# Equal-target matrices of two mean stages of a graph kernel: made once and kept in DRAM, with new orders for four stages

## What is computed

```python
edge_index = jnp.stack([src, dst])
h = jnp.maximum(_layernorm(x, axis=-1), 0.0)
x = x + _L0_gnn_ref(h, edge_index, edge_weight)
h = jnp.maximum(_layernorm(x, axis=-1), 0.0)
x = x + _L1_gnn_ref(h, edge_index, ...)     # two mean convolutions
h = jnp.maximum(_layernorm(x, axis=-1), 0.0)
x = x + _L2_gnn_ref(h, edge_attr_2, ..., edge_index)
h = jnp.maximum(_layernorm(x, axis=-1), 0.0)
x = x + _L3_gnn_ref(h, edge_index, ...)
```

```python
def _sage_conv(x, src, dst, W_l, W_r, b, num_nodes):
    msgs = x[src]
    agg = jax.ops.segment_sum(msgs, dst, num_segments=num_nodes)
    deg = jax.ops.segment_sum(jnp.ones((src.shape[0],), x.dtype), dst, num_segments=num_nodes)
    agg = agg / jnp.maximum(deg, 1.0)[:, None]
    return agg @ W_l.T + b + x @ W_r.T
```

## Time and profile before

| | us |
|---|---|
| median of 3 runs (5081.73 to 5089.31) | 5084.06 |
| the profiled execution | 5089.15 |
| its span, from the first to the last instruction | 5087.2 |
| setup and `gcn_phase`, in the span | 0 to 1262 |
| first mean stage | 1262 to 1956 |
| second mean stage | 1956 to 2623 |
| edge-MLP stage | 2623 to 3629 |
| `mean_phase` | 3629 to 4313 |
| `final_phase` | 4313 to 5087 |

### The profile page before, as it was taken

The page is one execution under the profiler, slowest core; times in us unless marked ns, Lnnn a source line. Parts: engine busy times, 40 slices in busy tenths (PEclk is TensorE's granted clock), DMA queues, the critical chain, the costliest instruction groups (busy, mean ns, idle before and its releaser), DMA issues. The chain is left out here.

```text
span 5087.2 us, 85226 instructions
## 1 busy us (share of the span) xinstructions
PE 3758.1 (74%) x21809; PEld 2963.0 (58%) x22119; DVE 4106.7 (81%) x20428; ACT 3646.0 (72%) x9165; POOL 3840.9 (76%) x3164
## 2 busy tenths in 40 slices
PE   6537787876767778988868788778778777766564
PEld 4326666655655666776646666566566565645443
DVE  7659999988999997877778888878699898756564
ACT  0048898987777777877768788788678786766564
POOL 7777888875777777888766777776578886777777
PEclk9868999998888889999989899999899898877777
DMA  8977777776666666776668888888456565333332
GB/s 252 320 215 212 191 197 200 204 188 151 166 156 154 153 139 148 166 157 155 135 160 249 241 242 245 231 238 205 123 134 138 132 144 104 102 93 94 95 96 68
DMA packets 837876, 864.12 MB, mean 170 GB/s; under 512 B 89656, under 2 KB 621174, under 8 KB 837382
## 3 DMA queue, kind: packets, MB, share of 16 engines
q1 hardware_dynamic: 512124, 566.02, 34.5%
q0 software_dynamic: 219520, 232.07, 26.6%
q10 hardware_dynamic: 105738, 60.56, 4.3%
HBM read 339.16 MB, written 523.51 MB: 170 GB/s over the span
## 5 line engine op out<-in xcount | busy, mean ns | idle before, releaser
L1238 POOL DMA_INDIRECT node<-sage_comb,leadd x392 | 639.4, 1631 | 184.0 <-DMA node<-sage_comb,leadd 89.1
L474 PE MATMUL dense_p<-ident,dense_h 128*128 128x128 f32 x1956 | 335.4, 299 | 362.1 <-ACT dense_h L468 352.7
L468 ACT ACTIVATE dense_h<-dense_x,dense_n_shift,dense_n_rstd 128x128 f32<-128x128 f32 x1304 | 533.8, 486 | 74.5 <-DVE dense_n_shift L457 73.7
L474 PEld LDWEIGHTS dense_p<-ident,dense_h 128*128 128x128 f32 x1956 | 235.8, 151 | 459.1 <-ACT dense_h L468 439.3
L1238 POOL DMA_INDIRECT sums<-mlp_same,leadh x196 | 327.6, 1671 | 136.9 <-issue 63.7
L484 PE MATMUL dense_p<-wT,dense_hT 128*128 128x128 f32 x2608 | 375.0, 291 | 51.7 <-ACT dense_hT L1076 21.8
L1238 POOL DMA_INDIRECT node<-gcn_comb,leads x196 | 325.5, 1661 | 98.0 <-issue 39.1
L1238 POOL DMA_INDIRECT sums<-mean_comb,leads x196 | 321.9, 1642 | 92.1 <-DMA sums<-mean_comb,leads 42.7
L484 PEld LDWEIGHTS dense_p<-wT,dense_hT 128*128 128x128 f32 x2608 | 376.6, 208 | 20.7 <-issue 6.2
L1073 ACT ACTIVATE dense_hT<-dense_p 128x512 f32<-128x512 f32 x489 | 284.9, 587 | 61.5 <-PE dense_p L474 60.7
L465 ACT ACTIVATE dense_n_std<-dense_n_mean_var,eps 128x4 f32<-128x4 f32 x652 | 188.4, 293 | 153.6 <-DVE dense_n_mean_var L451 150.1
(11 more groups left out here) (322 smaller groups left out, 13889.1 us busy)
## 6 DMA issues: line engine op xcount, KB each, us to landing
node<-b SPq DMA_DIRECT2D x392, 256.0 KB
sums<-zero_row SPq DMA_DIRECT2D x392, 256.0 KB
node<-zero_row ACTq DMA_DIRECT2D x49, 1152.0 KB, 15.0
dense_x<-in_x SPq DMA_DIRECT2D x163, 256.0 KB
out<-dense_y SPq DMA_DIRECT2D x163, 256.0 KB
x_src<-xs SPq DMA_DIRECT2D x49, 256.0 KB, 5.8
y_dst<-gcn_y SPq DMA_DIRECT2D x49, 256.0 KB, 3.5
sage_xs<-x_src SPq DMA_DIRECT2D x49, 256.0 KB
```

What stands on the lines that cost most here:

```text
L468: tiles(lambda t: nc.scalar.activation(out[:, t, :], x[:, t, :], func, bias=b.sh[:, t:t + 1], scale=b.rs[:, t:t + 1])).then_inc(done, 1)
L474: return tiles(lambda t: nc.tensor.transpose(ps[:, t * P:(t + 1) * P], x[:, t, :], ident))
L1238: pool.indirect_dma_start(table, bass.IndirectOffsetOnAxis(ap=leads[:, i * G + c, t:t + 1], axis=0), e.comb[c][:, t, :], None, element_off ...
```

## The change

The first mean stage gets a step `put_same` on SyncE after `match`: it stores the six matrices of a chunk (768 KB) in a new DRAM tensor `same_dst`. `lead` of the next round on the same buffer waits until that has landed. The second mean stage loses `spread`, `krow` and `match` and gets `get_same` on SyncE: the matrices of the next round's chunk are loaded once `combine` is done with the buffer, those of the first round at the stage's start. `combine` waits for the load. 49 stores and 49 loads of 768 KB are added, 38.5 MB each way.

```diff
@@ Tables
+        self.same = dram("same_dst", (NCH, P, (T + U) * HALF), F32)
@@ planner
-AHEAD = ("fetch", "get_keys", "get_xs", "get_h", "get_x", "get_g", "get_side")
+AHEAD = ("fetch", "get_same", "get_keys", "get_xs", "get_h", "get_x", "get_g", "get_side")
@@ sage1_phase
-                    Node("spread", TENSOR, 560), Node("krow", SCALAR, 500), Node("lead", VECTOR, 2500), ...
+                    Node("spread", TENSOR, 560), Node("krow", SCALAR, 500), Node("lead", VECTOR, 2500, after=(("put_same", 1, 0),)), ...
-                 + edge_tail(True, SCALAR, whole=True) + fill_nodes(FILL))
+                 + edge_tail(True, SCALAR, match_after=(("put_same", 1, 0),), whole=True)
+                 + [Node("put_same", SYNC, 1400, after=(("match", 0, 0),), main=False)] + fill_nodes(FILL))
+                if name == "put_same":
+                    sp.wait_ge(e.done[c], at.after(i, "match"))
+                    sp.dma_start(chunk_rows(tb.same, i, c), e.same[c][:, :, :].rearrange("p b q -> p (b q)")).then_inc(kept_same[c], 16)
+                sp.wait_ge(kept_same[c], RDS[c] * 16)
+                if name == "lead":
+                    wait_rounds(dve, kept_same[c], i, 16)
@@ sage2_phase
-                 + [Node("spread", TENSOR, 560), Node("krow", SCALAR, 500)]
-                 + edge_tail(True, VECTOR, whole=True) + fill_nodes(FILL))
+                 + [Node("combine", TENSOR, 2850, after=(("get_same", 1, 0),)), Node("sumT", VECTOR, 610), Node("apply", TENSOR, 1000),
+                    Node("keep", SCALAR, 590, after=(("add", 1, 0),)),
+                    Node("add", GPSIMD, 2 * ADD, after=(("keep", 0, 0),), main=False, adds="table"),
+                    Node("get_same", SYNC, 1400, after=(("combine", 0, 0),), main=False)] + fill_nodes(FILL))
+            def load_same(i, c):
+                sp.dma_start(e.same[c][:, :, :].rearrange("p b q -> p (b q)"), chunk_rows(tb.same, i, c)).then_inc(e.krow_in[c], 16)
+                if name == "get_same" and not is_last(i, c):
+                    sp.wait_ge(e.done[c], at.after(i, "combine"))
+                    load_same(i + 1, c)
             for c in L:
                 load_p(0, c)
+                load_same(0, c)
-                if name == "match":
-                    match_keys(nc, dve, k, e, i, c, KD, field(k, i, c, INVD))
-                if name == "krow":
-                    act.wait_ge(e.done[c], at.before(i, name))
-                    nc.scalar.activation(e.krow[c][:, :], e.p[c][:, :], ACT.Copy).then_inc(e.done[c], 1)
-                if name == "spread":
-                    pe.wait_ge(e.done[c], at.before(i, name))
-                    spread_keys(nc, k, e.p[c], i, c, KD).then_inc(e.done[c], 1)
                 if name == "combine":
+                    pe.wait_ge(e.krow_in[c], (i + 1) * 16)
@@ TIMES
-    "sage2": (90922, 38122, (
+    "sage2": (84249, 34447, (
```

7 lines of the change are left out of this document (4 added, 3 removed), and 253 rows, old and new, of the table TIMES.

## The result

The changed kernel is slower: **5104.1 us**, median of 5 runs (5091.38 to 5109.27), against 5084.06, a ratio of 1.0033 with a 95% interval of 1.0022 to 1.0044 (the two medians alone would give 1.0039). The forecast was 5073, 11 us less. The profiled execution took 5109.3 us, span 5107.5, which is 20.3 more than the span before.

What follows compares the result with a forecast made beforehand. GpSimd's queue was taken to bound the second mean stage, with other engines nearly full beside it elsewhere. First mean stage +3, second -5, edge-MLP -3, `mean_phase` -6: -11 us, from 5084 to 5073, range 5054 to 5105.

Steps and rivals of the forecast that it cites:

- What bounds the kernel: Second mean stage is GpSimd's queue from end to end; DVE, 520.6 of 667 us, is not what it waits for.
- The order's two gains in the second mean stage, -4 and -4: Second mean stage: two fewer uncovered landings in the tail, -4 us; shorter barrier wait behind the last addition, -4 us.
- The DMA term, +3 and +1: Added traffic makes GpSimd's additions take longer: +3 us in the second mean stage, +1 in the first.
- The additions' landing grows past its cover: Rival, 20%: mean stages' landings exceed the 5.2 us that four gathers cover; 5120 us, or 5095 if the first is spared.
- The first mean stage, +3: First mean stage: 9 more dense steps on nearly full DVE, +2 us, and added DMA traffic, +1.
- The edge-MLP stage, -3: Edge-MLP stage: -6.5 us for fewer dense steps and +3.5 against it, together -3.
- the -6.5 for 48 fewer dense steps: Edge-MLP stage: 48 fewer dense steps take 9.6 us off DVE, so GpSimd's queue moves faster, -6.5 us.
- the +3.5 against it: Edge-MLP stage: two more uncovered landings and a first addition 8 gathers earlier cost +3.5 us.
- `mean_phase`, -6: mean_phase: 28 fewer dense steps, -4 us, and one uncovered landing less, -2, together -6.
- 28 dense steps less are -4: mean_phase: losing 28 dense steps, 5.6 us of DVE, saves 4 us (0 to -5.6).
- The uncovered landing less (-2): mean_phase: one addition's landing fewer without gathers to cover it, -2 us.
- the first grows by more than 10 (the stores): Sign that the forecast is wrong: the first mean stage grows by more than 10 us, because of the stores.

Runs made afterwards that it cites:

- exchange_small: Kernel before with its orders; match, spread and krow left out of the second mean stage, stores and loads cut to 4 KB after the first round; ratio 0.9993.
- after_small: Changed kernel with its new orders, stores and loads cut from 768 KB to 4 KB from the second round on; 5083.48 against 5081.77 us, ratio 1.0003.
- traffic_double: Kernel before plus, per chunk, two stores in the first mean stage and one and a half loads in the second, read by nothing; 5132.30 us, ratio 1.0106.
- before_new34: Kernel before with the changed kernel's new due times in the edge-MLP stage and mean_phase alone; ratio 1.0200.
- loads_only: Kernel before plus five first-round stores and 49 loads of 768 KB in the second mean stage into buffers nothing reads; ratio 1.0021.
- traffic_only: Kernel before, its orders and arithmetic kept, plus the change's stores and loads into tiles nothing reads; 5100.55 against 5079.93 us, ratio 1.0043.

## Why the prediction was wrong, point by point

**What bounds the kernel** was right, and it was the step that mattered most for not expecting more. The second mean stage is GpSimd's queue: 93 us of DVE out of it moved it by 2 us (exchange_small). The DVE time after is 446 us, forecast 430: taking out instructions of 103.0 us shortened the busy time by 93 only, and the 67 dense steps more were 18 us, not 13.

**The order's two gains in the second mean stage, -4 and -4**, were right in size. Their sum shows in after_small: 666.9 to 657.9 is -9.0, of it -6.3 in GpSimd's part and -2.7 at the barrier. The split is less sure than the sum: the uncovered waits themselves are only 2 us less there, and GpSimd's instructions 5. The first addition stands at 1994.86, 31.9 us into the stage where before it stood 41.4 into it, and it came in time:

```profile
1994.86 1.62 POOL L1238 DMA_INDIRECT node<-sage_comb,leadd  x1 [0.30 <-DMA sage_a<-node,gsrc]
```

**The DMA term, +3 and +1, is the first of two steps that failed**: it was booked at 4 us and came to 15. The shares were foreseen a little high (0.83 and 0.85; measured 0.78 and 0.81). They rose by 13 and 15 points for 18 and 19 booked, so the 306 GB/s of the earlier trace rows was too slow for these transfers. By the 435 GB/s of "DMA: Bandwidth & Descriptors" of the Trainium skill ("Specifications"), which the prediction set aside, it would have been 13 points, an estimate, and the traces are nearer to that. What was wrong in the price was the currency. I priced the load by how much longer a GpSimd instruction would be, 196 x 0.044 us, and that did not change: 1627 ns before and after, 1612 to 1633 in the other kernels with this traffic or more, 1610 in after_small. The added traffic acts on the landing. It cost 13.6 us in the second mean stage (671.5 against 657.9) where +3 was booked. In the whole, 1.0033 against 1.0003 is 15 us for a term of 4.

**The rival "The additions' landing grows past its cover"** had the mechanism, the place and the point from which it decides, and I gave it 20%. My reason against it was the earlier trace rows: a share of 0.84 in the edge-MLP stage with "no jump" in the waits. That reading was poor. 63.7 us there against 29.5 is twice as much, and a mean share doesn't tell how its traffic lies: the edge-MLP stage has no transfer of 768 KB. And the 2.45 us that the rival set against its cover of 5.2 was read in the tail, where the DMA engines were at 0.46; the kernel before has uncovered waits of up to 5.1 us in its first mean stage. The rival's own price was too high, 0.5 us at 70 additions (35 us), since it made all landings late. (Its 5095 for the second stage alone is not what its terms give: 5073 + 20 + 6 = 5099.) In fact 8 of 40 are, by 1 us each; traffic_double has 17 of 38, by 1.2. The landings scatter, so there is no point at which all tip over: a fifth were past the cover while the others still came in time. Of the 7.3 us of the row above, "DMA: Bandwidth & Descriptors" of the Trainium skill ("Latency and other measured facts"), with its 0.2 us for an access to HBM on average and 2 us at high load, would have given 2.45 + 1.8 = 4.3, an estimate under the cover. The trace does not agree: late landings take 5.9 to 7.3 us here.

**The first mean stage, +3:** 694.0 to 696.5, +2.5, so the size came out, but by luck. In a single profile this stage can't be read to 3 us: before_new34 has 688.8 with the code of the kernel before, and after_small has 699.2 with stores of 4 KB. The barrier behind it, 9.0 us after for 3.6, is 7.7 to 9.0 in before_new34, loads_only and exchange_small too, which have before's order there, so it isn't the new order's. The stores, which cost 8.9 us of GpSimd's part in traffic_only, do not show there in the changed kernel (687.6, and 690.4 in after_small). `put_same` issues a store right behind `match`, and traffic_only later, behind a fill; that this is the reason was not tried.

**The edge-MLP stage, -3:** 1006.3 to 1007.3, and 1002.3 in after_small. Nine kernels with before's orders in the later stages, before among them, came out between 999.9 and 1010.2, so neither the -6.5 for 48 fewer dense steps nor the +3.5 against it can be told from nothing.

**`mean_phase`, -6, is the second step that failed, by its sign:** 684.0 to 693.8, and 692.1 in after_small, so the traffic is not it. The same nine lie here between 682.2 and 690.5, mean 686.0. Some 7 us are lost, 5 of them at the barrier, which takes 9.4 us in after and after_small and 3.7 to 5.6 in the nine. The timeline of all engines at the end of the stage after shows what it waits for, the last dense chunk, 28 steps fewer in the stage notwithstanding:

```profile
4324.66 1.55 POOL L1238 DMA_INDIRECT sums<-mean_comb,leads  x1 [0.30 <-DMA sums<-mean_comb,leads]
...
4330.88 0.69 DVE L1057 SCALAR_TENSOR_TENSOR dense_y<-dense_p,dense_y 128x512 f32<-128x512 f32 x1 [5.89 <-PE dense_p L483]
...
4335.60 1.02 POOL L625 DMA_INDIRECT final_s<-sums,gsrc  x1 [9.39 <-POOLq L929]
```

Before, the last dense operation (4308.53 to 4309.22) and the last addition (to 4308.98) end together. What failed is "28 dense steps less are -4": by this timeline the stage's end is set by when the last chain of dense steps is through, and removing steps elsewhere does not move that. No run tried it. The uncovered landing less (-2) doesn't show either: the waits labelled "issue" fell from 27.5 to 13.3 us, but all idle time before the additions only from 92.1 to 86.7, and GpSimd's part of the stage didn't shrink.

**Sum.** Forecast: orders and arithmetic -15, traffic +4. Measured: orders and arithmetic +2 (1.0003, interval -3 to +7), traffic +15. So 17 us of the miss are in the first and 11 in the second, and either alone would have taken away the gain. Of the 17, `mean_phase` has the most (-6 forecast, +8 in after_small); the rest is spread over stages whose single profiles don't tell it. Of "What would show it", the second mean stage within 15 us of 667 and at 92% or more of GpSimd's queue, the duration of additions and the edge-MLP stage held; `mean_phase` at 678, DVE at 430 and a share of 0.8 in the first mean stage (0.78) did not. The sign "the first grows by more than 10 (the stores)" looked at the wrong stage: in the changed kernel it was above all the loads of the second.

No version that beats both kernels was found. The best with the arithmetic gone and next to no traffic, which is more than any real version could have, is 0.9993 (0.9982 to 1.0004).

## What to carry to other kernels

Before trading arithmetic for DMA traffic, ask which engine's queue sets the stage: here 93 us of DVE time were worth nothing that could be measured, since they were not on GpSimd's queue. Then price the traffic by the landings that something waits for, not by the busy share or by instruction time: list each wait for a landing, the cover ahead of it (four gathers, 5.2 us) and the landing, and look at the DMA share of the place where the landing was read (here 2.5 us at 0.46). A factor of two between them was thin here when transfers of 768 KB were added. A table of due times is part of a stage's input state, and a change in one stage wants new tables behind it, whose own end (the barrier) has to be looked at.

## What the runs showed of the hardware

- From the end of an indirect DMA that adds to DRAM to the start of the next one that waits for its landing, it took 2.4 to 2.7 us in the tail of the second mean stage (before, DMA share 0.46), 2.4 to 5.1 in the first mean stage of the same kernel, and up to 7.3 us (after, share 0.95 around it) and 8.3 (loads_only) beside loads of 768 KB. In the mean stages of all kernels here, GpSimd's own time for issuing it stayed at means of 1.61 to 1.64 us, and its 0.30 us between two indirect DMAs stayed too, at DMA shares from 0.65 to 0.85.
- Where ScalarE and GpSimd waited for the same landing, GpSimd's indirect DMA started 0.73 us after ScalarE's instruction (22 waits, 0.732 to 0.734 us).
- The price of the loads grew faster than the bytes: +8.6 us of GpSimd's part of the second mean stage for 38.5 MB, +19.6 for 57.8 MB. For the stores of the first (+8.9 and, for 77.1 MB, +25.1) profiles of the same code differ too much to tell.
- With one store and then two of each chunk the DMA share of the first mean stage went from 0.65 to 0.76 and 0.85; waits for landings had doubled by then (29.5, 37.8, 62.6 us). Shares well under 1 already cost time.
